# One-hot planes made for half a pair at once, and groups and matrices cut by chunk, in a graph network on one core

## The chip, the cores and the metric
One core of one Trainium2 chip runs the whole kernel. The metric is the device time of one execution in microseconds. A change is judged by the median of several executions of each kernel.

## The reference
A graph of 3125 nodes with 128 features has 103125 edges (src, dst), sorted by dst, each with a weight and six attributes. Four blocks follow each other, each ending in a layer normalisation of x plus the block's output:

```
0: h = x + segsum(x[src], dst);      out = x @ Wres + bres + relu(h @ W1 + b1) @ W2 + b2
1: twice: h + mean over edges of h[src], then two linear maps and a relu
2: four steps: x + 0.1 * tanh(x @ A.T + neighbours(x @ W_phi.T) + self + bias)
   neighbours: sum over edges of dinv[src] * dinv[dst] * edge_weight * h[src]
3: relu(segsum((x @ W + b)[src] + (edge_attr @ We + be), dst))
```

That is eight sums over the edges of the same graph: 1 + 2 + 4 + 1.

## The kernel before
The kernel turns the edges into two dense 3125 x 3125 matrices once: counts (fp16) and weights (float32), with the self loops taken in. Each of the eight sums is then a dense product on TensorE. The nodes are laid out as node = 25 p + k, with p one of 125 partitions and k one of NC = 25 chunks. A chunk of destinations is 125 columns of a matrix; a source chunk k is 125 rows.

**Build.** A pair is two destination chunks (PAIRS = 13, the last one half empty). For a pair every one of 125 destinations t has up to 64 slots of edges for each of its two chunks, on 128 partitions. VectorE makes one-hots in `produce`: `hot_hi`, 128 wide, from the source's partition (L660), `eq`, LO = 26 wide, from its chunk (L658), and eq times the two halves of the weight (L665, two multiplies). All are fp16. This goes in STEPS = 4 steps of 34, 33, 33 and 25 destinations; two buffers alternate, so step u waits (`sums_ok`) until TensorE has used step u - 2. TensorE (`pair`, L1304) multiplies hot_hi by the three narrow planes, four small products for a destination, in UNITS = 15 units of 8 or 9 destinations, and between the units it does the sums of round 0 for the pair before, ten products at a time (`sum_counts`, L1279). ScalarE (`leave`, L962 and L964) copies each unit out of one of three PSUM slots to a staging buffer, counts and weights. There are two staging buffers. SyncE's queue (L391 to L401) waits for the counts of a pair and stores them in `count_mats` (L395), waits for the weights and stores them in `weight_mats` (L398), waits until both have landed and only then hands the buffer back with `stg_free`, for which ScalarE waits at the start of a pair. The pairs are a loop: the first is written out on TensorE, the other twelve are a loop body.

**Rounds.** Round 0 has its sums from the build and goes through product1, product2, normalisation and transposes, group by group. In the seven others TensorE runs `aggregate` for one group of destination chunks after another: GROUPS = 7 groups, six of GRP = 4 chunks (500 columns, one PSUM bank) and one of one chunk. Layers 1 and 3 (rounds 1, 2, 7) read the counts in fp16 (L1183): 25 source chunks, each as a high and a low part, so 50 products a group; ten of them, then product1 of the group before, ten more, product2 of the group before, twenty in a loop whose addresses come from registers, and the last ten. The four rounds of layer 2 (3 to 6) read the weights in float32 (L1193): 25 products, which the trace shows as 50 passes. The matrices come from DRAM through a ring of four slots, two pairs (four chunks) to a load; a weight group is two loads (source chunks 0 to 12 and 12 to 25). SyncE issues load i when item i - 4 is used; the first load of round 7, in a counts slot over two weight slots, waits for one item more (`over_w`). The first group of a round waits for the results of all groups of the round before, piece by piece (`need_parts`). VectorE does `first_sum` and `finish`, ScalarE tanh, square roots and the copies of the transposes.

The code's order is written out by hand; nothing is planned by a scheduler.

Of the kernel before, what the change touches and what calls it, by code (L numbers as in the profile page):

```python
# [31 lines left out]
NODES = 3125  # L32
EDGES = 103125
D = 128
# [19 lines left out]
STEPS = len(STEP_AT) - 1  # L54
SUM_BANK = 7
GRP = 4
GROUPS = -(-NC // GRP)
# [20 lines left out]
def chunks_of(g):  # L78
    return min(GRP, NC - GRP * g)
# [6 lines left out]
def build_program(nc, x, edge_pairs, edge_w, dst_blocks, edge_feats, w, out):  # L86

    ctx = ExitStack()
    with ctx:
# [7 lines left out]
        count_mats = nc.dram_tensor("count_mats", (PAIRS, 128, NC * 2 * NP), F16).ap()  # L97
        weight_mats = nc.dram_tensor("weight_mats", (PAIRS, 128, NC * 2 * NP), F32).ap()
# [95 lines left out]
        stg_c = [at(37500 * i, 128, [NC, 2 * NP], F16) for i in range(2)]  # L194
        stg_w = [at(37500 * i + 12500, 128, [NC, 2 * NP]) for i in range(2)]
# [16 lines left out]
        ring_c = [at(25000 * i, 128, [2, NC, 2 * NP], F16) for i in range(RING)]  # L212
        ring_w = [at(50000 * (i // 2) + (24000 if i % 2 else 0), 128, [2, W_KS[i % 2][1] - W_KS[i % 2][0], 2 * NP])
# [6 lines left out]
        Cn = at(128992, NP, [GROUPS * GRP, D])  # L220
# [129 lines left out]
        def _(sp):  # L350
# [17 lines left out]
            def store_out(g):  # L368
# [3 lines left out]
                sp.dma_start(out.rearrange("(p c) f -> p c f", c=NC)[:, GRP * g:GRP * g + n, :],  # L372
# [14 lines left out]
            def fast_loads():  # L387
# [5 lines left out]
                with sp.Fori(0, PAIRS) as q:  # L393
                    sp.wait_ge(counts_out, UNITS * q + UNITS)
                    sp.dma_start(count_mats[bass.ds(q, 1)].rearrange("a p n -> (a p) n"),  # L395
                                 stg_all[:, bass.ds(q % 2, 1), 0:STG_C // 2].bitcast(F16).rearrange("p a n -> p (a n)")).then_inc(mats_out, 16)
                    sp.wait_ge(weights_out, UNITS * q + UNITS + OUT_PAD)
                    sp.dma_start(weight_mats[bass.ds(q, 1)].rearrange("a p n -> (a p) n"),  # L398
                                 stg_all[:, bass.ds(q % 2, 1), STG_C // 2:].rearrange("p a n -> p (a n)")).then_inc(mats_out, 16)
# [6 lines left out]
                full = NC // GRP  # L406
                sp.dma_start(inv_deg[:, 0:full, 0:GCOL],
                             row[:, 0:full * GCOL].rearrange("o (g n) -> o g n", n=GCOL).to_broadcast([D, full, GCOL])).then_inc(inv_in, 16)
                sp.dma_start(inv_deg[:, full, 0:NODES - full * GCOL],
                             row[:, full * GCOL:].to_broadcast([D, NODES - full * GCOL])).then_inc(inv_in, 16)  # L410
# [93 lines left out]
        def _(dve):  # L504
# [140 lines left out]
            def produce(q, u):  # L645
# [4 lines left out]
                def code(cols, wide):  # L650
                    return cols.rearrange("p q t j -> p (q t) j").unsqueeze(2).to_broadcast([128, n, wide // 2, 2])
# [773 lines left out]
```

## Time and profile before

| | |
|---|---|
| time, median of 3 | 1177.41 us (1174.58 to 1179.05) |
| profiled execution, its time and its span | 1174.85 us, 1173.0 us |
| granted TensorE clock, mean | 0.96 |
| TensorE busy | 1044.1 us (89%) |
| VectorE busy | 543.5 us (46%) |
| ScalarE busy | 274.7 us (23%) |
| moved by DMA | 310.57 MB, 265 GB/s on the mean |
| chain that ended last | TensorE 75%, DMA 12%, VectorE 5% |

Times inside the span are us from its start. The build lies between about 88 and 312, round 0 between 312 and 343; the float32 rounds are from 501 to 1083, the last round ends at 1173. Busy shares are means over these stages, which have different limits. The granted clock is a share of 2.4 GHz.

### The profile page before, as it was taken

Reading aid. Unit: us, or ns where it says so; the run is one execution under the profiler, and the core shown is the slowest. Engines: PE = TensorE matmul, PEld = TensorE weight load, DVE = VectorE, ACT = ScalarE, POOL = GpSimd, SP = SyncE. Lnnn points to the kernel's source line nnn. Section 1 sums busy time; section 2 is a strip of 40 time slices with the busy share of each in tenths; the row PEclk is TensorE's granted clock in tenths of the full one; section 3 lists DMA queues with packets and bytes.
Section 4 is the critical chain, followed back from the end, with each engine's and each line's share of the span. In section 5 each row is a group of like instructions: output and inputs, shape, how many; then the busy total and the mean of one; then the engine's idle time right before and its main releaser. Section 6 shows DMA issues by size and latency. Waiting matters only on the chain.

```text
span 1173.0 us, 25340 instructions
## 1 busy us (share of the span) xinstructions
PE 1044.1 (89%) x10553; PEld 619.7 (53%) x10553; DVE 543.5 (46%) x1061; ACT 274.7 (23%) x558; POOL 67.8 (6%) x69
## 2 busy tenths in 40 slices
PE   0335888888869999999999999999999999999998
PEld 0234677777655555545445554465544645445454
DVE  4398799999473336522312223222322314444333
ACT  0246698888520000000000000000000002112100
POOL 3811000000000000000000000000000000000000
PEclk9865799999999999999999999999999999999999
DMA  6405476767798675777766987669886698753951
GB/s 190 104 12 157 202 299 287 300 287 300 328 367 349 236 303 222 268 304 312 262 254 227 386 354 284 233 247 382 337 305 222 258 385 324 306 203 145 427 193 31
DMA packets 40520, 310.57 MB, mean 265 GB/s; under 512 B 12138, under 2 KB 15069, under 8 KB 18581
## 3 DMA queue, kind: packets, MB, share of 16 engines
q1 hardware_dynamic: 29528, 299.34, 65.0%
q0 software_dynamic: 8416, 9.50, 2.9%
q10 hardware_dynamic: 2522, 0.98, 0.4%
q8 instruction: 38, 0.62, 0.2%
q14 instruction: 16, 0.13, 0.0%
HBM read 244.49 MB, written 65.26 MB: 264 GB/s over the span
## 4 chain that ended last, share of the span: by engine, by line
PE 75%; DMA 12%; DVE 5%; issue 3%; ACT 2%; ACTq 2%; SPq 0%; DVEq 0%
PE ps L1193 45%; PE ps L1183 17%; DMA weight_mats<-arena 11%; PE ps L1142 4%; PE ps L1304 2%; PE ps L1279 2%; PE ps L1097 2%; PE ps L1155 1%; ACTq L908 1%; DMA edge_table<-arena 1%; ACTq L911 1%; DVE arena L665 1%; PE ps L1124 0%; DVE stats L673 0%; ACT arena L930 0%
## 5 line engine op out<-in xcount | busy, mean ns | idle before, releaser
L1193 PE MATMUL ps<-arena 125*128 125x500 f32 (+1 forms) x700 | 268.5, 539 | 0.0
L1193 PE MATMUL ps<-arena,parts_even 125*128 125x500 f32 (+1 forms) x700 | 267.6, 538 | 0.0
L1193 PEld LDWEIGHTS ps<-arena 125*128 125x128 f32 x700 | 123.3, 190 | 127.8 <-issue 127.8
L1193 PEld LDWEIGHTS ps<-arena,parts_even 125*128 125x128 f32 x700 | 122.9, 189 | 127.4 <-issue 127.4
L948 ACT ACTIVATE XT<-ps 128x500 f32<-128x500 f32 (+1 forms) x49 | 26.6, 543 | 517.8 <-PE ps L1155 517.8
L1183 PE MATMUL ps<-arena 125*128 125x500 f16 (+2 forms) x700 | 140.8, 352 | 3.8 <-issue 3.2
L1304 PE MATMUL ps<-arena 64*128 64x52 f16 (+1 forms) x6500 | 106.5, 181 | 36.5 <-DVE arena L665 21.7
L962 ACT ACTIVATE arena<-ps 128x400 f16<-128x400 f32 (+1 forms) x195 | 124.1, 636 | 38.6 <-PE ps L1304 24.0
L1304 PEld LDWEIGHTS ps<-arena 64*128 64x128 f16 x6500 | 96.4, 95 | 54.3 <-ACT arena L964 30.8
L964 ACT ACTIVATE arena<-ps 128x400 f32<-128x400 f32 (+1 forms) x195 | 116.6, 598 | 0.0
L660 DVE TENSOR_TENSOR arena<-arena 128x4224 f16<-128x4224 f16 (+2 forms) x52 | 116.2, 2235 | 0.0
L784 DVE TENSOR_TENSOR arena<-ps,dinv 125x512 f32<-125x512 f32 (+1 forms) x28 | 17.8, 634 | 197.0 <-PE ps L1142 197.0
L742 DVE COPY arena<-ps 128x500 f32<-128x500 f32 (+1 forms) x28 | 17.4, 621 | 186.5 <-PE ps L1193 186.5
L1183 PEld LDWEIGHTS ps<-arena 125*128 125x128 f16 (+1 forms) x700 | 64.6, 96 | 72.0 <-issue 6.7
L1279 PE MATMUL ps<-arena,parts_even 125*128 (+1 forms) x650 | 86.2, 283 | 2.3 <-ACT x_buf L970 1.8
L497 POOL DMA_INDIRECT arena<-in_edge_feats,ptr x25 | 31.1, 1245 | 886.9 <-DVE S L812 860.8
L1183 PE MATMUL ps<-arena,parts_even 125*128 125x500 f16 (+2 forms) x350 | 71.1, 354 | 0.6 <-issue 0.4
L1279 PEld LDWEIGHTS ps<-arena,parts_even 125*128 125x128 f16 x650 | 60.9, 101 | 12.3 <-ACT arena L962 1.9
L665 DVE TENSOR_TENSOR arena<-arena 128x858 f16<-128x858 f16 (+2 forms) x104 | 55.4, 574 | 0.0
L1183 PEld LDWEIGHTS ps<-arena,parts_even 125*128 125x128 f16 (+1 forms) x350 | 32.8, 97 | 34.1 <-issue 1.7
L1020 ACT ACTIVATE arena<-arena 125x512 f32<-125x512 f32 (+1 forms) x28 | 16.3, 584 | 136.6 <-DVE arena L787 136.6
L658 DVE TENSOR_TENSOR arena<-arena 128x858 f16<-128x858 f16 (+2 forms) x52 | 30.2, 580 | 21.4 <-PE ps L1304 20.5
(176 smaller groups left out, 710.6 us busy)
## 6 DMA issues: line engine op xcount, KB each, us to landing
arena<-weight_mats SPq DMA_DIRECT2D x24, 3250.0 KB, 11.4
arena<-weight_mats SPq DMA_DIRECT2D x24, 3000.0 KB, 10.9
arena<-count_mats SPq DMA_DIRECT2D x18, 3125.0 KB, 13.2
weight_mats<-arena SPq DMA_DIRECT2D x13, 3125.0 KB, 14.4
count_mats<-arena SPq DMA_DIRECT2D x13, 1562.5 KB, 6.0
arena<-weight_mats SPq DMA_DIRECT2D x4, 1625.0 KB, 7.2
arena<-weight_mats SPq DMA_DIRECT2D x4, 1500.0 KB, 6.3
arena<-count_mats SPq DMA_DIRECT2D x3, 1562.5 KB, 6.2
```

Source lines behind the costliest of these rows:

```text
L497: nc.gpsimd.indirect_dma_start(attrs[c % 3].rearrange("p s t -> p (s t)"), None, feats_v, bass.IndirectOffsetOnAxis(ptr8[:, c:c + 1], 1)). ...
L658: v.tensor_tensor(eq, numbers(iota_lo, LO), code(lo_c[:, bass.ds(q, 1), t0:t0 + n, :], LO), ALU.is_equal).then_inc(eq_ok, 1)
L660: v.tensor_tensor(hot_hi[b][:, 0:n, :].rearrange("p t (a j) -> p t a j", j=2), numbers(iota_hi, 128), code(hi_c[:, bass.ds(q, 1), t0:t0 + ...
L665: ins = v.tensor_tensor(to, eq, code(w_c[:, bass.ds(q, 1), t0:t0 + n, k, :], LO), ALU.mult)
L948: s.activation(XT[:, GCOL * g:GCOL * g + n], ps[:, 6 + q % 2, 0:n], ACT.Copy).then_inc(xt_ready, 1)
L962: s.activation(stg_c[odd].rearrange("p k (j t) -> p k j t", j=2)[:, :, :, cols], sums_of(u, 0), ACT.Copy).then_inc(counts_out, 1)
L964: s.activation(stg_w[odd].rearrange("p k (j t) -> p k j t", j=2)[:, :, :, cols], sums_of(u, 1), ACT.Copy).then_inc(weights_out, 1)
L1142: ins = t.matmul(o, a, b[:, :], start=(i == 0 and r != 7), stop=(i == len(terms) - 1), skip_group_check=(r == 7))
L1183: ins = t.matmul(o, lhs, rhs, start=(not loop and k == 0 and j == 0), stop=(not loop and k == NC - 1 and j == 1))
L1193: ins = t.matmul(o, xs[:, k, :], rhs, start=(k == 0), stop=(k == NC - 1))
L1279: ins = t.matmul(o, parts_even[:, j, k, :], counts[:, 2 * NP * k:2 * NP * k + 2 * NP], start=(k == 0 and j == 0), stop=(k == NC - 1 and j ...
L1304: ins = t.matmul(ps[:, bank + j, o + (LO if a else 0):o + 2 * LO], hot_hi[b][rows, e, :], hot_lo[b][rows, e, LO * a:LO * z], start=(T == U ...
```

## The change
- `produce` makes the narrow planes for half a pair (67 and 58 destinations) instead of for a step: one comparison, then one multiply that writes both weight planes, reading eq once for each plane. hot_hi is still made by steps. The order on VectorE is now: wait for the buffers of step 2h, eq of half h, hot_hi of step 2h, multiply of half h (step 2h is then ready), wait for the buffer of step 2h + 1, hot_hi of that step.
- `hot_lo` holds three planes [3, destinations, 26], one buffer for each half; TensorE reads the first two as two pieces of 26.
- The matrices in staging and DRAM are by chunk: [2 chunks, 25, 125] for a pair, where they were [25, 250]. The rows of a store are two pieces of half the length; a load takes up to four chunks, each a piece of its own. Products read pieces of 125 columns where they read 250.
- The groups are 4, 4, 4, 4, 4, 3, 2 chunks. 25 chunks are loaded for a round, where it was 13 pairs.

```diff
+HALF_AT = STEP_AT[::2]
-GROUPS = -(-NC // GRP)
+GROUP_AT = (0, 4, 8, 12, 16, 20, 23, NC)
+GROUPS = len(GROUP_AT) - 1
...
-        count_mats = nc.dram_tensor("count_mats", (PAIRS, 128, NC * 2 * NP), F16).ap()
+        count_mats = nc.dram_tensor("count_mats", (PAIRS, 2, 128, NC * NP), F16).ap()
...
-        hot_hi = [at(75000 + 14008 * i, 128, [STEP_MAX, 128], F16) for i in range(2)]
-        hot_lo = [at(83704 + 14008 * i, 128, [STEP_MAX, 3 * LO], F16) for i in range(2)]
+        hot_hi = [at(75000 + 8704 * i, 128, [STEP_MAX, 128], F16) for i in range(2)]
+        HALF_MAX = max(z - a for a, z in zip(HALF_AT, HALF_AT[1:]))
+        hot_lo = [at(92408 + 10452 * i, 128, [3, HALF_MAX, LO], F16) for i in range(2)]
...
-            def produce(q, u):
-
-                t0, n, b = STEP_AT[u], STEP_AT[u + 1] - STEP_AT[u], u % 2
-                eq = hot_lo[b][:, 0:n, 0:LO].rearrange("p t (a j) -> p t a j", j=2)
+            def produce(q, half):
...
-                used = UNITS_TO[u - 2] - (UNITS if u < 2 else 0)
-                dve.wait_ge(sums_ok, UNITS * q + used + SUMS_PAD)
-                v.tensor_tensor(eq, numbers(iota_lo, LO), code(lo_c[:, bass.ds(q, 1), t0:t0 + n, :], LO),
-                                ALU.is_equal).then_inc(eq_ok, 1)
-                v.tensor_tensor(hot_hi[b][:, 0:n, :].rearrange("p t (a j) -> p t a j", j=2), numbers(iota_hi, 128),
-                                code(hi_c[:, bass.ds(q, 1), t0:t0 + n, :], 128), ALU.is_equal)
-                dve.wait_ge(eq_ok, STEPS * q + u + 1)
-                for k in range(2):
-                    to = hot_lo[b][:, 0:n, LO + LO * k:2 * LO + LO * k].rearrange("p t (a j) -> p t a j", j=2)
-                    ins = v.tensor_tensor(to, eq, code(w_c[:, bass.ds(q, 1), t0:t0 + n, k, :], LO), ALU.mult)
-                ins.then_inc(hots_ok, 1)
+                def wait_used(u):
+
+                    used = UNITS_TO[u - 2] - (UNITS if u < 2 else 0)
+                    dve.wait_ge(sums_ok, UNITS * q + used + SUMS_PAD)
+
+                def rows_hot(u):
+                    t0, n = STEP_AT[u], STEP_AT[u + 1] - STEP_AT[u]
+                    return v.tensor_tensor(hot_hi[u % 2][:, 0:n, :].rearrange("p t (a j) -> p t a j", j=2),
+                                           numbers(iota_hi, n, 128), code(hi_c[:, bass.ds(q, 1), t0:t0 + n, :], 128),
+                                           ALU.is_equal)
+
+                t0, n, u = HALF_AT[half], HALF_AT[half + 1] - HALF_AT[half], 2 * half
+                eq = hot_lo[half][:, 0, 0:n, :]
+                wait_used(u)
+                v.tensor_tensor(eq.rearrange("p t (a j) -> p t a j", j=2), numbers(iota_lo, n, LO),
+                                code(lo_c[:, bass.ds(q, 1), t0:t0 + n, :], LO), ALU.is_equal).then_inc(eq_ok, 1)
+                rows_hot(u)
+                dve.wait_ge(eq_ok, 2 * q + half + 1)
+                both = w_c[:, bass.ds(q, 1), t0:t0 + n, :, :].rearrange("p q t k j -> p (q t k) j")
+                v.tensor_tensor(hot_lo[half][:, 1:3, 0:n, :].rearrange("p k t m -> p t k m"),
+                                eq.unsqueeze(2).to_broadcast([128, n, 2, LO]),
+                                both.unsqueeze(2).to_broadcast([128, 2 * n, LO // 2, 2]), ALU.mult).then_inc(hots_ok, 1)
+                wait_used(u + 1)
+                rows_hot(u + 1).then_inc(hots_ok, 1)
...
-                            if n == GCOL:
-                                rhs = slot[:, :, ks, :].rearrange("p q a n -> p q (a n)")
-                            else:
-                                rhs = slot[:, 0:1, ks, 0:NP].rearrange("p q a n -> p (q a n)")
+                            rhs = slot[:, 0:chunks_of(g), ks, :].rearrange("p c a n -> p c (a n)")
...
-                                                   hot_lo[b][rows, e, LO * a:LO * z],
+                                                   hot_lo[half][rows, a:z, e_lo, :],
```

## Rows read from the trace of the kernel before
**Rows 1.** The page, part 4: share of the chain by line.
```profile
PE ps L1193 45%; PE ps L1183 17%; DMA weight_mats<-arena 11%; PE ps L1142 4%; PE ps L1304 2%; PE ps L1279 2%; PE ps L1097 2%; PE ps L1155 1%; ACTq L908 1%; DMA edge_table<-arena 1%; ACTq L911 1%; DVE arena L665 1%; PE ps L1124 0%; DVE stats L673 0%; ACT arena L930 0%
```
**Rows 2.** Timeline of SyncE's queue: start, duration, what (idle before, releaser).
```profile
133.73 0.35 SPq L395 DMA_DIRECT2D count_mats<-arena  x1
...
292.92 0.34 SPq L395 DMA_DIRECT2D count_mats<-arena  x1
```
**Rows 3.** The chain in order of time, one pair: start, duration, what.
```profile
214.65 14.42 DMA weight_mats<-arena
```
**Rows 4.** Timeline of the build, VectorE, TensorE and ScalarE around 211 us.
```profile
210.31 1.14 DVE L665 TENSOR_TENSOR arena<-arena 128x884 f16<-128x884 f16 x2
...
211.59 0.63 PE L1304 MATMUL ps<-arena 64*128 64x52 f16 x36 [1.34 <-DVE arena L665]
...
212.26 1.24 PE L1279 MATMUL ps<-arena,parts_even 125*128 x10
...
213.45 0.62 ACT L962 ACTIVATE arena<-ps 128x450 f16<-128x450 f32 x1 [1.51 <-SPq L401]
...
214.57 0.62 PE L1304 MATMUL ps<-arena 64*128 64x52 f16 x36 [0.16 <-ACT arena L964]
...
215.35 0.60 DVE L658 TENSOR_TENSOR arena<-arena 128x858 f16<-128x858 f16 x1
...
218.14 1.11 DVE L665 TENSOR_TENSOR arena<-arena 128x858 f16<-128x858 f16 x2
```
**Rows 5.** Groups by form, VectorE's one-hots: busy us, mean ns of one.
```profile
L660 DVE TENSOR_TENSOR arena<-arena 128x4224 f16<-128x4224 f16 x26 | 61.1, 2351 | 0.0
...
L660 DVE TENSOR_TENSOR arena<-arena 128x4352 f16<-128x4352 f16 x13 | 31.5, 2420 | 0.0
...
L660 DVE TENSOR_TENSOR arena<-arena 128x3200 f16<-128x3200 f16 x13 | 23.6, 1818 | 0.0
...
L658 DVE TENSOR_TENSOR arena<-arena 128x884 f16<-128x884 f16 x13 | 8.1, 620 | 2.3 <-PE ps L1304 1.6 <-DVE W_rep L823 0.4
L658 DVE TENSOR_TENSOR arena<-arena 128x650 f16<-128x650 f16 x13 | 6.5, 499 | 10.0 <-PE ps L1304 9.9
```
**Rows 6.** Timeline, TensorE in the second pair and around 195 us.
```profile
123.09 0.35 PE L1304 MATMUL ps<-arena 64*128 64x26 f16 x10 [2.97 <-issue]
...
195.43 0.63 PE L1304 MATMUL ps<-arena 64*128 64x52 f16 x36 [1.56 <-ACT arena L964]
...
195.99 2.27 PE L1279 MATMUL ps<-arena,parts_even 125*128 x10
```
**Rows 7.** Windows: PE, PEld, DVE, ACT, POOL busy; clock, DMA share, GB/s.
```profile
196.00:200.00 4.00, 4.00 (x117) 3.10 (x113) 3.11 (x3) 2.09 (x5) 0.00 (x0) 0.58 0.35 147
...
332.00:336.00 4.00, 2.18 (x16) 1.53 (x15) 3.46 (x16) 1.32 (x3) 0.00 (x0) 1.00 1.02 434
...
502.00:1078.00 576.00, 576.00 (x1854) 298.09 (x1853) 167.01 (x320) 45.01 (x70) 26.68 (x22) 1.00 0.74 284
```
**Rows 8.** Timeline, end of round 6 and start of round 7.
```profile
1075.21 8.86 SPq L422 DMA_DIRECT2D arena<-count_mats  x4
...
1079.19 3.96 PE L1193 MATMUL ps<-arena,parts_even 125*128 125x125 f32 x34
...
1085.69 3.24 PE L1183 MATMUL ps<-arena 125*128 125x500 f16 x10 [2.54 <-issue]
```
**Rows 9.** The page, part 6: KB of one transfer, median us to landing.
```profile
arena<-weight_mats SPq DMA_DIRECT2D x24, 3000.0 KB, 10.9
```
**Rows 10.** The chain in order of time, a float32 group and an fp16 group.
```profile
1014.64 17.61 PE ps L1193 x42
...
1142.19 10.56 PE ps L1183 x50
```
**Rows 11.** Timeline, the looped products of round 1's last group.
```profile
420.56 2.73 PE L1183 MATMUL ps<-arena 125*128 x20 [0.41 <-issue]
```
**Rows 12.** Timeline, the last full group's scaling.
```profile
1166.34 1.11 DVE L682 TENSOR_SCALAR arena<-arena,mv,rstd 125x128 f32<-125x128 f32 x4
```

More of the change, by code:

```diff
@@ L78, in chunks_of, with groups_to @@
 def chunks_of(g):
-    return min(GRP, NC - GRP * g)
+    return GROUP_AT[g + 1] - GROUP_AT[g]
+def groups_to(k):
+    return sum(a < k for a in GROUP_AT[:-1])
 def layer_of(r):
@@ L211, in build_program @@
         RING = 4
-        ring_c = [at(25000 * i, 128, [2, NC, 2 * NP], F16) for i in range(RING)]
-        ring_w = [at(50000 * (i // 2) + (24000 if i % 2 else 0), 128, [2, W_KS[i % 2][1] - W_KS[i % 2][0], 2 * NP])
+        ring_c = [at(25000 * i, 128, [GRP, NC, NP], F16) for i in range(RING)]
+        ring_w = [at(50000 * (i // 2) + (24000 if i % 2 else 0), 128, [GRP, W_KS[i % 2][1] - W_KS[i % 2][0], NP])
                   for i in range(RING)]
@@ L641, in _, with numbers @@
             v.tensor_copy(mode[:, :], ps[0:1, 6, 0:1]).then_inc(mode_ok, 1)
-            def produce(q, u):
-                t0, n, b = STEP_AT[u], STEP_AT[u + 1] - STEP_AT[u], u % 2
-                eq = hot_lo[b][:, 0:n, 0:LO].rearrange("p t (a j) -> p t a j", j=2)
+            def produce(q, half):
                 def code(cols, wide):
+                    n = cols.shape[2]
                     return cols.rearrange("p q t j -> p (q t) j").unsqueeze(2).to_broadcast([128, n, wide // 2, 2])
-                def numbers(row, wide):
+                def numbers(row, n, wide):
@@ L825, in fast @@
                 with dve.Fori(0, PAIRS) as q:
-                    for u in range(STEPS):
-                        produce(q, u)
+                    for half in range(2):
+                        produce(q, half)
                 dve.wait_ge(sq_ok, 1)
@@ L1220, in aggregate @@
                     pe.wait_ge(slot_in[(i + 1) % RING], 16 * ((i + 1) // RING + 1))
-                    for k in range(12, NC, GRP):
-                        need_parts(r, g, min(k + GRP, NC))
-                        ins = weight_steps(slot, 1, range(k, min(k + GRP, NC)))
+                    for a, z in zip(GROUP_AT[3:], GROUP_AT[4:]):
+                        need_parts(r, g, z)
+                        ins = weight_steps(slot, 1, range(a, z))
                     ins.then_inc(item_used, 1)
@@ L1300, in pair @@
                             o, e = 2 * LO * (T - UNIT_AT[u]), T - STEP_AT[step]
+                            half = step // 2
+                            e_lo = T - HALF_AT[half]
                             for a, z in ((0, 2), (2, 3)):
```

100 lines of the change are left out of this document (51 added, 49 removed).

## The prediction, written before the changed kernel had run
> **What bounds the kernel now.** I read the chain of waits first. Nearly half of the span is TensorE in L1193 (the four float32 rounds) and 17% in L1183 (the fp16 rounds); 11% is one transfer, weight_mats<-arena [rows 1]. So there are two stages: the build of the matrices, in 13 passes called pairs, up to about 306 us, and then eight rounds in which TensorE is hardly ever idle. The change touches both.
>
> In the build, SyncE's queue issues the store of a pair's counts every (292.92 - 133.73) / 10 = 15.92 us; the weights' store follows, and the chain waits 14.42 us for it [rows 2, 3]. The rest of the 15.92 is queue work, and ScalarE begins a pair only when the earlier store is in: 1.51 us of idle before the copy at 213.45 [rows 4]. So it is the store that sets the pace.
>
> The timeline of one pair shows what is right behind it: a circle between VectorE and TensorE. VectorE makes the one-hots of a step (33 or 34 of the 125 columns), TensorE multiplies the step's four units and frees the buffer, and VectorE may then make the step after next. With S0 to S3 for the four steps of a pair: S0 is ready at 210.31 + 1.14 = 211.45; TensorE starts 0.14 later and ends unit 3 at 214.57 + 0.62 = 215.19; VectorE begins S2 at 215.35; its last operation ends at 218.14 + 1.11 = 219.25 [rows 4].
>
> **Build, old circle.** Durations are from the rows by form [rows 5]. Between the starts of L658 and L665 lie 218.14 - 215.35 = 2.79 us for operations of 0.60 and 2.35 us, so each next operation starts 0.08 before the recorded end of the last. S2 needs 3.90 us (0.60 + 2.35 + 1.11 - 0.16), S0 needs 0.62 + 2.42 + 1.14 - 0.16 = 4.02. TensorE needs 3.58 us from S0 ready to unit 3 done (3.74 less the 0.16 for ScalarE in the last row), so 3.5 from S2 ready to unit 11 done. With 0.16 from TensorE to VectorE, twice, the circle is 3.58 + 0.16 + 3.90 + 3.52 + 0.16 + 4.02 = 15.3 us. It fits under 15.92 with 0.6 us to spare.
>
> **Build, new circle.** Two halves (67 and 58 columns) replace the four steps for the narrow planes. Removed for a pair: two comparisons of the narrow planes and six of the eight multiplies; the rows_hot operations stay as they are. VectorE's own work falls: eight operations fewer, each with a fixed cost (620 ns for 884 elements, 499 for 650: 0.52 ns an element, so 0.16 fixed, less the overlap of 0.08), 8 x 0.08 = 0.65 us. But the first step of a half now waits for the planes of both steps. At 0.52 ns an element (the wide rows give the same: 2351 - 1818 ns over 1024):
> - comparison of 67 x 26 = 1742 elements: 0.62 + 858 x 0.52 = 1.07 us; of 1508: 0.94;
> - both planes in one multiply, 3484 elements: 1.82 + 284 x 0.52 = 1.97 us; 3016: 1.72.
> So S0 is ready after 1.07 + 2.42 + 1.97 - 0.16 = 5.30 us instead of 4.02, and S2 after 0.94 + 2.35 + 1.72 - 0.16 = 4.85 instead of 3.90. The waits before them are not moved: half 0 still waits for unit 11 of the pair before, half 1 for unit 3. The circle: 3.58 + 0.16 + 4.85 + 3.52 + 0.16 + 5.30 = 17.57 us. S1 and S3 come soon enough (one rows_hot behind S0 and S2), and VectorE is idle in the circle although it has less to do. TensorE waits some 0.7 us before unit 8, and before unit 0 over 2 us (from unit 11 to unit 0 pass 0.16 + 5.30, and units 12 to 14 with their sums fill less than 3 of it). ScalarE (15.92 less its 1.51 of idle, 14.4 us of copies) and the store (15.9) then have slack; that covers also what smaller pieces in the store might cost, up to 1.6 us a pair.
>
> 17.57 - 15.92 = 1.65 us for each of the ten pairs at this pace: 16.5 us. The first two pairs are slower in any case: the clock is at 1.2 GHz and TensorE stands for the code of its loop, as at 123.09 with 2.97 us [rows 6]. There the later first S0 costs 1.3 and the two longer half-productions a part of 2 x (1.28 + 0.95): between 1.3 and 5.8, I take 2.9, because part hides behind the code stalls. Build: +19.4.
>
> **The granted clock.** After a gap of 1.34 us it held in the pair above; after one of 1.56 us TensorE fell to 1.2 GHz (0.58 granted on the mean from 196 to 200), and the ten sums took 2.27 us instead of 1.24 [rows 4, 6, 7]. Today the slack of the pair hides that. In the new circle it would not: about +1.4 us each time (1.0 for the sums, the rest in the units), and the gap before unit 0 is longer. In round 0, where TensorE works 2.18 of 4 us, the full 2.4 GHz held [rows 7], so the bounds are 0 and 12 x 1.4 = 17 us; I take 2, one or two falls.
>
> **Rounds.** Groups of 4,4,4,4,4,3,2 chunks replace six of 4 and one of 1.
> - *End of round 6.* The first matrix of round 7 lies over both weight slots and is loaded only when group 5 is done: issued at 1075.21; TensorE then has the one-chunk group, ends at 1079.19 + 3.96 = 1083.15, and stands 2.54 us until 1085.69; the trace calls it issue, but 1085.69 is 10.5 us behind the load's issue, and loads of about that size land after 10.9 us on the median. The first ten are then slow, 3.24 us where 2.11 is normal (50 take 10.56) [rows 8 to 10]. A last group of two chunks gives 50 x 0.21 = 10.5 us and products: the load is hidden. -2.5 and -1.1 = -3.6.
> - *Float32 passes.* 500 columns take 17.61 / 42 = 0.419 us (34 of the 42 are of this group), 125 columns (3.96 - 0.16) / 34 = 0.112, 0.16 of it the end of the last [rows 8, 10]; a pass over all columns but 2000 costs 0.531 now and 0.524 as 375 + 250 in proportion. 0.007 x 50 x 4 rounds = -1.4.
> - *fp16 passes.* 20 narrow ones in the register-addressed loop take 2.73 us [rows 11], 0.14 to 0.2 each where 0.053 is their share of 0.211. That floor hits now two groups: 375 columns want 0.158 (a loss of up to 0.04 x 20), 250 want 0.106 (0.09 x 20), against 0.14 x 20 before: -0.2 to +1 a round; I take +0.9, three rounds: +2.7. The sources are now pieces of 125 with odd fp16 offsets; no row has that, so nothing to +10 us, I take nothing, as in the nearest row, where 500 columns in two pieces of 250 take 0.211 [rows 10].
> - *Loads* have the same bytes in pieces half as long. The transfer engines are 74% busy in the float32 rounds [rows 7] and each load has four slots' time: hidden until they take a third longer.
> - *Round 0* ends with shorter VectorE work for group 5: -0.8. *Tail:* one chunk more in the last normalisation, 0.28 for the scaling (1.11 for four) [rows 12] and as much again for each other operation: +1.
> Rounds: -3.6 - 1.4 + 2.7 - 0.8 + 1.0 = -2.1.
>
> Sum: 19.4 + 2 - 2.1 = +19.3. The profiled execution took 1174.85 us (span 1173.0); the median of three is 1177.41, 2.6 above it. I forecast 1174.85 + 19.3, and half of the 2.6, as 1195.
>
> The Trainium skill ("VectorE: DVE Perf Modes", the section on the TRN2 errata) says that each VectorE instruction on SBUF pays a fixed latency and advises larger tiles to pay it less often. The rows agree on the fixed part (0.16 us a record) [rows 5]. By that rule the change should speed the build; it is rival A, and the circle is why I don't follow it.
>
> **Rivals.**
> A. *VectorE's total is the bound, or the store stays it.* If waits between the two engines overlap more than I read, the pair stays at 15.92 and only the rounds count: 1177.4 - 2 to - 5, so 1174; if VectorE's saving of 0.65 us a pair also went through, 8 us more, 1166. For it: from 210.31 to 219.25 VectorE has no idle time. Against it: ScalarE's 1.51 us behind the store, which no VectorE saving removes [rows 4]. It decides if S0 to S0 stays under 15.92. Chance 0.15.
> B. *The clock falls in nearly every pair.* 17 us instead of 2: 1210. For it: the gap of over 2 us; against it: round 0. Chance 0.2.
> C. *The combined multiply is not at two elements a cycle.* Its source repeats a row for both planes, which no row shows. At twice the time an element (1.04 ns) the two cost 3.4 us a pair more, 12 pairs: 1236. Chance 0.05.
>
> The Trainium skill ("Vector Engine (DVE) Microarchitecture Reference", section 5.1) lists what lets a two-source operation take pairs: 2-byte types and an innermost step of 1; a row read again is allowed. By that C should not happen; no run here shows it yet.
>
> **How the numbers follow.** Forecast 0.6, A 0.15, B 0.2, C 0.05. The forecast's own range is 1186 to 1204 (start of the build 1.3 to 5.8, fp16 passes, circle 16.9 to 17.9). Leaving out C, the end of B and the better part of A: 1176 to 1213. A change within 0.5% (6 us) can't be told from none: A counts half as same and half as faster: slower 0.84, same 0.08, faster 0.08.
>
> **What would show it.** Stores of the counts 17 to 18 us apart; SyncE no longer the one that ScalarE waits for; TensorE waiting over 2 us for the combined multiply before unit 0; the multiply at 1.97 us; no stall at the start of round 7. Wrong if the stores still come every 16 us, if VectorE has no idle time in the build, or if the multiply takes over 3 us.

## The result and the profile after

| | before | after |
|---|---|---|
| median | 1176.89 us (4 runs, 1174.58 to 1179.05) | 1200.6 us |
| ratio | | 1.0193, 95% interval 1.0164 to 1.0223 |
| profiled execution, time and span | 1174.85, 1173.0 us | 1202.75, 1200.9 us |
| last count store of the build issued | 308.46 | 337.82 |
| end of the build (last sums of round 0) | 311.83 | 345.51 |
| start of the first fp16 group of round 1 | 343.36 | 379.62 |
| granted clock, mean | 0.96 | 0.945 |

Slower by 1.9%; 1.0193 of 1176.9 is 1199.6. (A fourth execution of after, of 1321.96 us at a clock of 0.84, is outside the ratio; with it the median of four reads 1200.6.)

The chain by line, to be held against [rows 1]. The transfer weight_mats<-arena, 11% there, is gone from it. VectorE's multiply has grown from 1% (L665) to 4% (L683), TensorE's units from 2% (L1304) to 6% (L1321), the sums of round 0 from 2% (L1279) to 5% (L1294).

```profile
PE ps L1208 44%; PE ps L1201 17%; PE ps L1321 6%; PE ps L1294 5%; PE ps L1163 5%; DVE arena L683 4%; PE ps L1118 2%; PE ps L1176 1%; ACTq L929 1%; DMA edge_table<-arena 1%; ACTq L932 1%; PE ps L1145 0%; DVE stats L694 0%; ACT arena L985 0%; DMA arena<-in_edge_w 0%
```

SyncE's queue of after, the stores of the counts; it answers to [rows 2], where they came every 15.9 us. From 136.51 to 337.82 they come every 201.31 / 11 = 18.30 us, and one interval, 154.71 to 171.70, is 16.99.

```profile
136.51 0.39 SPq L402 DMA_DIRECT2D count_mats<-arena  x1
154.71 0.38 SPq L402 DMA_DIRECT2D count_mats<-arena  x1
171.70 0.38 SPq L402 DMA_DIRECT2D count_mats<-arena  x1
190.41 0.38 SPq L402 DMA_DIRECT2D count_mats<-arena  x1
...
337.82 0.38 SPq L402 DMA_DIRECT2D count_mats<-arena  x1
```

VectorE of after in that pair [rows 4, 5]: start, duration, what, in brackets the idle time before it and what ended it. VectorE stands twice a pair, each time for TensorE, with four operations in each half where it had eight.

```profile
150.88 1.07 DVE L678 TENSOR_TENSOR arena<-arena 128x1742 f16<-128x1742 f16 x1 [1.67 <-PE ps L1321]
151.86 2.42 DVE L671 TENSOR_TENSOR arena<-arena 128x4352 f16<-128x4352 f16 x1
154.20 1.96 DVE L683 TENSOR_TENSOR arena<-arena 128x3484 f16<-128x3484 f16 x1
...
159.61 0.95 DVE L678 TENSOR_TENSOR arena<-arena 128x1508 f16<-128x1508 f16 x1 [1.18 <-PE ps L1321]
...
162.74 1.72 DVE L683 TENSOR_TENSOR arena<-arena 128x3016 f16<-128x3016 f16 x1
...
167.87 1.07 DVE L678 TENSOR_TENSOR arena<-arena 128x1742 f16<-128x1742 f16 x1 [1.67 <-PE ps L1321]
```

TensorE of after, start of three pairs. Before unit 0 it stands 3.05 us for L683, each time; at 156.30 the clock holds (ten sums in 1.25 us), in the next two pairs it doesn't (2.26 us).

```profile
156.30 0.62 PE L1321 MATMUL ps<-arena 64*128 64x52 f16 x36 [3.05 <-DVE arena L683]
156.85 1.25 PE L1294 MATMUL ps<-arena,parts_even 125*128 x10
158.03 1.43 PE L1321 MATMUL ps<-arena 64*128 64x52 f16 x100
...
164.59 1.02 PE L1321 MATMUL ps<-arena 64*128 64x52 f16 x68 [0.85 <-DVE arena L683]
...
173.29 0.81 PE L1321 MATMUL ps<-arena 64*128 64x52 f16 x36 [3.05 <-DVE arena L683]
174.03 2.26 PE L1294 MATMUL ps<-arena,parts_even 125*128 x10
...
191.99 0.68 PE L1321 MATMUL ps<-arena 64*128 64x52 f16 x36 [3.05 <-DVE arena L683]
192.59 2.26 PE L1294 MATMUL ps<-arena,parts_even 125*128 x10
```

Two windows of after, columns as in [rows 7]: the build has a mean clock of 0.88, and the stretch around that gap 0.50.

```profile
155.00:300.00 145.00, 115.70 (x4400) 96.38 (x4400) 111.94 (x64) 110.48 (x247) 0.00 (x0) 0.88 0.64 265
...
172.00:176.00 4.00, 2.71 (x46) 2.02 (x46) 3.42 (x2) 1.09 (x3) 0.00 (x0) 0.50 0.86 350
```

End of round 6 in after: the stall of [rows 8] is gone, and the first ten products of round 7 take 2.29 us, not 3.24. But inside the first group of round 7 there is a new wait of 1.29 us, for VectorE's results of the last group, which now has two chunks.

```profile
1106.05 7.34 PE L1208 MATMUL ps<-arena,parts_even 125*128 125x250 f32 x34
1113.23 2.29 PE L1201 MATMUL ps<-arena 125*128 125x500 f16 x10
...
1124.41 4.43 PE L1201 MATMUL ps<-arena 125*128 125x500 f16 x20 [1.29 <-DVE arena L718]
```

**Where the 27.9 us between the two profiled spans are.** From the tables of both traces:

| stretch | us |
|---|---|
| before the first of the stores that count (133.73, 136.51) | +2.8 |
| eleven pairs at 16.99 instead of (308.46 - 133.73) / 11 = 15.88 | +12.2 |
| the same pairs beyond 16.99 (lower clock) | +14.4 |
| last pair: in before its counts were ready some 2.2 us before SyncE, waiting for the earlier store, issued theirs; in after there is no such slack | +2.6 |
| last fifty sums (7.21 instead of 5.54, lower clock) | +1.7 |
| round 0, from its first product (33.6 instead of 31.0) | +2.6 |
| rounds 1 and 2 (154.3 instead of 158.15) | -3.9 |
| rounds 3 to 6 | -2.3 |
| stall at the start of round 7 | -2.5 |
| round 7 | +0.3 |

The profiled execution of after, 1202.75 us, is the slowest of the three in the ratio (the others took 1196.62 and 1198.45), so these 27.9 us are more than the 22.7 of the ratio. Two of the rows are falls of the clock that come and go from one profile to the next: in the kernel with one more operation beside the circle (below), whose build is otherwise the same, the last fifty sums take 5.54 us and round 0 takes 31.3.

### The profile page after: what moved, and what is told of

It is laid out like the page before. It is cut to its first block, busy times and chain, and to the rows that moved or that the text cites. A ratio compares the mean times of both kernels' runs of the same rounds, so it can differ in the third digit from the quotient of the medians.

```text
span 1200.9 us, 25107 instructions
## 1 busy us (share of the span) xinstructions
PE 1053.9 (88%) x10553; PEld 645.3 (54%) x10553; DVE 536.1 (45%) x957; ACT 276.6 (23%) x558; POOL 68.5 (6%) x69
## 4 chain that ended last, share of the span: by engine, by line
PE 81%; DVE 8%; issue 5%; ACT 2%; ACTq 2%; DMA 1%; DVEq 0%; SPq 0%
PE ps L1208 44%; PE ps L1201 17%; PE ps L1321 6%; PE ps L1294 5%; PE ps L1163 5%; DVE arena L683 4%; PE ps L1118 2%; PE ps L1176 1%; ACTq L929 1%; DMA edge_table<-arena 1%; ACTq L932 1%; PE ps L1145 0%; DVE stats L694 0%; ACT arena L985 0%; DMA arena<-in_edge_w 0%
## 5 line engine op out<-in xcount | busy, mean ns | idle before, releaser
L1208 PE MATMUL ps<-arena,parts_even 125*128 125x500 f32 (+2 forms) x700 | 267.5, 537 | 0.0
L1208 PE MATMUL ps<-arena 125*128 125x500 f32 (+2 forms) x700 | 267.5, 537 | 0.0
L1321 PE MATMUL ps<-arena 64*128 64x52 f16 (+1 forms) x6500 | 106.8, 183 | 59.0 <-DVE arena L683 52.8
L969 ACT ACTIVATE XT<-ps 128x500 f32<-128x500 f32 (+2 forms) x49 | 26.6, 542 | 511.3 <-PE ps L1176 511.3
L1201 PE MATMUL ps<-arena 125*128 125x500 f16 (+3 forms) x700 | 139.6, 352 | 1.7 <-DVE arena L718 1.3
L1321 PEld LDWEIGHTS ps<-arena 64*128 64x128 f16 x6500 | 97.1, 97 | 77.6 <-issue 52.4
L805 DVE TENSOR_TENSOR arena<-ps,dinv 125x512 f32<-125x512 f32 (+2 forms) x28 | 17.8, 634 | 202.5 <-PE ps L1163 202.5
L1294 PE MATMUL ps<-arena,parts_even 125*128 (+1 forms) x650 | 96.9, 305 | 1.9 <-ACT x_buf L991 1.9
L763 DVE COPY arena<-ps 128x500 f32<-128x500 f32 (+2 forms) x28 | 17.4, 623 | 175.6 <-PE ps L1208 175.6
L1294 PEld LDWEIGHTS ps<-arena,parts_even 125*128 125x128 f16 x650 | 65.2, 108 | 16.6 <-ACT arena L983 2.0
L1201 PE MATMUL ps<-arena,parts_even 125*128 125x500 f16 (+3 forms) x350 | 70.6, 352 | 0.3 <-issue 0.3
L678 DVE TENSOR_TENSOR arena<-arena 128x1742 f16<-128x1742 f16 (+1 forms) x26 | 26.2, 1007 | 54.6 <-PE ps L1321 54.1
L683 DVE TENSOR_TENSOR arena<-arena 128x3484 f16<-128x3484 f16 (+1 forms) x26 | 47.9, 1843 | 0.0
L1041 ACT ACTIVATE arena<-arena 125x512 f32<-125x512 f32 (+2 forms) x28 | 16.4, 584 | 136.4 <-DVE arena L808 136.4
```

What stands on the lines that cost most here:

```text
L678: v.tensor_tensor(eq.rearrange("p t (a j) -> p t a j", j=2), numbers(iota_lo, n, LO), code(lo_c[:, bass.ds(q, 1), t0:t0 + n, :], LO), ALU. ...
L683: v.tensor_tensor(hot_lo[half][:, 1:3, 0:n, :].rearrange("p k t m -> p t k m"), eq.unsqueeze(2).to_broadcast([128, n, 2, LO]), both.unsque ...
L969: s.activation(XT[:, NP * GROUP_AT[g]:NP * GROUP_AT[g] + n], ps[:, 6 + q % 2, 0:n], ACT.Copy).then_inc(xt_ready, 1)
L1201: ins = t.matmul(o, lhs, rhs, start=(not loop and k == 0 and j == 0), stop=(not loop and k == NC - 1 and j == 1))
L1208: ins = t.matmul(o, xs[:, k, :], rhs, start=(k == 0), stop=(k == NC - 1))
L1294: ins = t.matmul(o, parts_even[:, j, k, :], counts[:, :, k, :], start=(k == 0 and j == 0), stop=(k == NC - 1 and j == 1), skip_group_check ...
```

## The experiments

Two theories were on the table. *Circle*: VectorE and TensorE wait for each other, and every microsecond between a freed buffer and the next S0 or S2 lengthens the pair; the clock falls in the gap this opens on TensorE. *Total*: the combined operations themselves, VectorE's sum of work or the new layout cost the time. The measured ratios are to the kernel before, run on the same chip in the same job.

| kernel | median us | ratio, 95% interval |
|---|---|---|
| half-pair planes alone | 1204.77 | 1.0247 (1.0221 to 1.0274) |
| changed kernel | 1200.6 | 1.0193 (1.0164 to 1.0223) |
| changed, one more operation beside the circle | 1199.42 | 1.0203 (1.0178 to 1.0228) |
| changed, the same operation on the circle | 1225.93 | 1.0432 (1.0405 to 1.0459) |
| changed, gap filled | 1183.52 | 1.0067 (1.0048 to 1.0087) |
| layout by chunk alone | 1180.68 | 1.0036 (1.0021 to 1.0052) |
| layout and groups, four old steps | 1172.22 | 0.9970 (0.9958 to 0.9982) |
| changed, narrow planes early | 1169.13 | 0.9941 (0.9920 to 0.9962) |
| before, two stores in flight | 1172.98 | 0.9971 (0.9956 to 0.9986) |
| early planes, two stores | 1168.66 | 0.9932 (0.9909 to 0.9955) |
| early planes, two stores, gap filled | 1161.82 | 0.9882 (0.9863 to 0.9900) |

### The change taken apart

**The one-hots back to four steps.** `produce` and the buffers are those of before, all else is the changed kernel:

```diff
-                    for half in range(2):
-                        produce(q, half)
+                    for u in range(STEPS):
+                        produce(q, u)
```

> The changed kernel with its one-hots made by four steps a pair again, as before; the groups of 4,4,4,4,4,3,2 chunks and the matrices by chunk stay. Theory (the circle between VectorE and TensorE, lengthened by the half-pair planes, is what costs in the build): the counts' stores come 15.9 us apart again (18.3 in the changed kernel), the build ends at 312, and the rounds keep what they gained (some 5.8 us between the end of the build and the last instruction): 1176.9 - 5.8 = 1171 us, 0.995 of before. Rival (the pieces of half the length in the stores, or the counts read back as two pieces with odd offsets in the sums, slow the build): the stores stay 17 us or more apart and the time is 1190 or more.

Measured: 1172.22 us, 0.997. The counts' stores are (312.58 - 135.77) / 11 = 16.07 us apart. So the build's loss is the half-pair production's, and the rest of the change is a small gain. The stores are still 0.2 us a pair further apart than in before, which is the layout's doing (next run).

**The groups back too.**

```diff
-GROUP_AT = (0, 4, 8, 12, 16, 20, 23, NC)
+GROUP_AT = (0, 4, 8, 12, 16, 20, 24, NC)
```

> The same with the groups of before too (six of 4 chunks and one of 1), so that of the change only the matrices' layout by chunk is left. If the rounds' gain is the groups' alone: the stall of 2.54 us at the start of round 7 is back, rounds 1 and 2 take 158.2 us instead of 154.3, and the time is that of before, 1176 to 1178, ratio 0.999 to 1.001. If the layout brings part of it (the gain in rounds 1 and 2): 1172 to 1174, ratio 0.997.

Measured: 1180.68 us, 1.0036: neither case. The layout by itself is no gain but costs 0.0036 x 1175.5 = 4.2 us, and the groups are then worth (1.0036 - 0.9970) x 1175.5 = 7.8 us by the ratios (8.5 by the medians), not 5.8. The pieces do cost: the stores are (311.12 - 134.27) / 11 = 16.08 us apart (15.88 in before), fifty fp16 products of 500 columns in four pieces of 125 take 10.66 us (10.56 in two of 250 [rows 10]), 42 float32 passes 17.64 (17.61). A fifty in the chain of this kernel:

```profile
1122.39 10.66 PE ps L1189 x50
```

**The half-pair planes alone.** The kernel before with the new `produce` and its buffers, layout and groups as they were.

```diff
-                    for u in range(STEPS):
-                        produce(q, u)
+                    for half in range(2):
+                        produce(q, half)
...
-                                                   hot_lo[b][rows, e, LO * a:LO * z],
+                                                   hot_lo[half][rows, a:z, e_lo, :],
```

> The kernel before with the half-pair planes and combined multiplies alone; layout and groups of before. Circle theory: stores 18.3 us apart, TensorE waits 3 us for the combined multiply before unit 0 and its clock falls in nearly every pair; the build ends at 345 and the rounds gain nothing: 1200.6 + 5.8 = 1206 us, 1.025 of before. Rival (the loss needs the new layout): below 1190 us.

Measured: 1204.77 us, 1.0247, stores (335.53 - 134.26) / 11 = 18.30 us apart. 2.5% of loss by this part, less the 0.3% that the others bring, is 2.2%; the whole change measured 1.9%, with overlapping intervals. The theory that the loss needs the layout is out.

### Circle or total

**One operation more, beside the circle.** `spare` is a cell that nothing reads.

```diff
                 rows_hot(u + 1).then_inc(hots_ok, 1)
+                v.tensor_reduce(spare, hi_c[:, 0:3, :, :].rearrange("p q t j -> p (q t j)"), AX, ALU.max)
```

> The changed kernel with one more VectorE operation (a reduction that nothing reads, an estimated 0.86 us) behind the last operation of each half, where VectorE then waits for TensorE: two a pair, some 1.7 us of VectorE work. Circle theory: it lies in VectorE's idle time (1.2 and 1.7 us) and moves nothing, 1200 us, 1.020 of before, at most 3 us more. Rival (VectorE's total is the bound in the build): 1.7 us for each of twelve pairs, 1220, 1.038.

Measured: 1199.42 us, 1.0203 (changed kernel 1.0193). VectorE works 1.86 us more in each pair (0.93 an operation) and nothing gets longer. Its timeline shows where they went: 0.82 us of idle time are left of 1.67.

```profile
182.78 0.93 DVE L689 TENSOR_REDUCE arena<-arena 128x1 f16<-128x750 f16 x1
184.53 1.07 DVE L679 TENSOR_TENSOR arena<-arena 128x1742 f16<-128x1742 f16 x1 [0.82 <-PE ps L1323]
```

**The same operation on the circle.**

```diff
+                v.tensor_reduce(spare, hi_c[:, 0:3, :, :].rearrange("p q t j -> p (q t j)"), AX, ALU.max)
                 dve.wait_ge(eq_ok, 2 * q + half + 1)
```

> The same operation put in front of the combined multiply instead, inside the circle, two a pair. Circle theory: each pair is longer by the whole of both, 1.7 us (pairs 17.0 to 18.3 become 18.7 to 20.0): 12 x 1.7 = 20 us more than the changed kernel, 1220 us, 1.037 of before. Rival (VectorE's total): as with the operation behind the half, whatever that gives.

Measured: 1225.93 us, 1.0432, so 0.0229 x 1176.8 = 27 us more than beside the circle, where 20 were expected. The same work costs nothing or 27 us by its place alone. The stores come (361.55 - 137.68) / 11 = 20.35 us apart, beside the circle (336.25 - 136.21) / 11 = 18.19. Of these 2.16 us a pair 1.7 are the operations' own; the other 0.5, some 5 us in eleven pairs, go with the clock: the gap before unit 0 is now 3.05 + 0.84 = 3.89 us, the clock falls behind it in all eleven pairs (in nine of eleven beside the circle), and in this one the second ten sums are slow as well.

```profile
180.83 0.81 PE L1323 MATMUL ps<-arena 64*128 64x52 f16 x36 [3.89 <-DVE arena L685]
181.57 2.26 PE L1296 MATMUL ps<-arena,parts_even 125*128 x10
...
185.63 1.90 PE L1296 MATMUL ps<-arena,parts_even 125*128 x10
```

**The circle cut.** The narrow planes are made ahead of the wait for hot_hi's buffer; for their own buffer they wait (`wait_lo`) for the unit of the pair before that read it last, 7 or 14.

```diff
-                wait_used(u)
+                wait_lo()
...
-                rows_hot(u)
                 dve.wait_ge(eq_ok, 2 * q + half + 1)
...
-                                both.unsqueeze(2).to_broadcast([128, 2 * n, LO // 2, 2]), ALU.mult).then_inc(hots_ok, 1)
+                                both.unsqueeze(2).to_broadcast([128, 2 * n, LO // 2, 2]), ALU.mult)
+                wait_used(u)
+                rows_hot(u).then_inc(hots_ok, 1)
```

> The changed kernel, but the narrow planes of a half are made before the wait for the buffer of the wide one-hots: they wait only for the units that read the half's own planes in the pair before (unit 7 for half 0, unit 14 for half 1), and only the 2.42 or 2.35 us of the wide one-hots are left between TensorE and S0 or S2. Circle theory: the circle falls from 17.0 to some 12 us (3.58 + 0.16 + 2.35 + 3.52 + 0.16 + 2.42), and the store is the bound again: counts' stores 16.0 us apart, the clock at 1.00, 1170 to 1172 us, 0.996 of before, as with the four old steps. VectorE's total (14.15 us busy a pair) stays below the store's 16.0, so its 0.65 us a pair less is worth nothing. Rival (it is the combined operations themselves, or VectorE's total, that cost): stores 17 us or more apart, 1185 or more.

Measured: 1169.13 us, 0.9941; stores (308.82 - 131.77) / 11 = 16.10 us apart. The same combined operations, in another order, cost nothing: it is not what they take, it is where they stand. The circle is not as short as expected, though. From a timeline of the kernel with two stores (below): unit 7 frees hot_hi's second buffer, VectorE then has the last step's rows, both planes of the next pair and its first rows to do, 222.32 to 229.5, and only then can unit 0 start; TensorE needs the other 7.5 us to its next unit 7. That circle is 15 us (the 12 us expected had looked at hot_hi's first buffer alone).

### What the clock costs

**The gap filled.** Ten products that nothing reads, in the 3.05 us in which TensorE stands.

```diff
                         if UNIT_AT[u] == STEP_AT[step]:
+                            if u == 0 and counts is not None:
+                                for _ in range(10):
+                                    t.matmul(ps[:, 6, 0:500], parts_even[:, 0, 0, :],
+                                             parts_even[:, 1, 0:4, 0:125], start=True, stop=True)
```

> The changed kernel plus ten fp16 products of 500 columns (0.21 us each, 2.1 us in all) into a free bank of PSUM before unit 0 of pairs 1 to 12, in the 3 us in which TensorE stands there. They are work beside the reference's. If the clock's fall is a cost of its own on top of the circle: granted 1.00 throughout, the ten sums at 1.25 us instead of 2.20, a pair at 17.0 us instead of 18.3, 13 to 16 us less than the changed kernel: 1185 to 1188, 1.008 of before. If the fall costs nothing beside the circle (VectorE would be waited for all the same), or if it comes from something else than the gap: 1200, as the changed kernel, or a few us more.

Measured: 1183.52 us, 1.0067, so (1.0193 - 1.0067) x 1176.9 = 14.8 us less than the changed kernel. Stores (322.91 - 136.09) / 11 = 16.98 us apart, every one; sums at 1.25 us; granted clock 1.00 where it was 0.88. TensorE does 2.1 us more a pair and the pair is 1.3 us shorter. A timeline of this kernel:

```profile
202.62 2.29 PE L1313 MATMUL ps<-parts_even 125*128 125x500 f16 x10
205.60 0.62 PE L1325 MATMUL ps<-arena 64*128 64x52 f16 x36 [0.70 <-DVE arena L683]
206.16 1.25 PE L1294 MATMUL ps<-arena,parts_even 125*128 x10
```

And a window of it, as the first of after above, with the clock at 1.00:

```profile
155.00:300.00 145.00, 131.36 (x4834) 104.36 (x4827) 121.05 (x69) 119.23 (x266) 0.00 (x0) 1.00 0.71 292
```

### What lies behind the store

**Two stores in flight, in the kernel before.** SyncE hands a staging buffer back when the store of the pair before has landed, not its own; one semaphore for each buffer, and the 13 passes written out.

```diff
-                    sp.wait_ge(mats_out, 32 * q + 32)
-                    sp.sem_inc(stg_free, 1)
+                    if q:
+                        sp.wait_ge(landed[(q - 1) % 2], 32 * ((q + 1) // 2))
+                        sp.sem_inc(stg_free, 1)
```

> The kernel before with the stores of two pairs in flight and nothing else: the old circle by itself. The prediction gave it as 15.3 us a pair right behind the store's 15.92. If so: stores of the counts 15.3 us apart, a gain of 0.6 for each of ten pairs, 1171 us, 0.995 of before. If the circle was read too short (16 or more): no gain, 1177. If it was read too long (waits between the engines overlap more): the pair falls to ScalarE's 14.5, 1163, 0.988.

Measured: 1172.98 us, 0.9971; stores (304.25 - 133.76) / 11 = 15.50 us apart, of two kinds: 15.0 (seven) and 16.3 to 16.4 (four). SyncE is gone from ScalarE's waits, so the store did set the pace; what lies right behind it is 15.0, not the 15.3 of the prediction. In three of the seven pairs of 15.0 us TensorE stands before unit 0 for VectorE (1.30 to 1.35 us), in the other four for ScalarE's copy L968 (1.44 to 1.53). So the old circle between VectorE and TensorE is no longer than 15.0 us, but this run doesn't show that it alone sets them.

```profile
211.37 0.32 SPq L397 DMA_DIRECT2D count_mats<-arena  x1
226.44 0.32 SPq L397 DMA_DIRECT2D count_mats<-arena  x1
242.82 0.32 SPq L397 DMA_DIRECT2D count_mats<-arena  x1
```

The longer kind is again the clock's: behind a gap of 1.55 us the ten sums take 2.27.

```profile
226.91 0.63 PE L1308 MATMUL ps<-arena 64*128 64x52 f16 x36 [1.55 <-ACT arena L968]
227.47 2.27 PE L1283 MATMUL ps<-arena,parts_even 125*128 x10
```

**Early planes and two stores.** The same edit on top of the early planes:

```diff
+                wait_lo()
...
+                        sp.wait_ge(landed[(q - 1) % 2], 32 * ((q + 1) // 2))
```

> The same with the stores of two pairs in flight: SyncE lets ScalarE have a staging buffer when the store of the pair before is in, not its own pair's, with a semaphore for each of the two buffers; its 13 passes are written out. If what makes the pair 16.0 us is that the store must land before the next is issued: ScalarE's copies (13.9 us busy a pair, 14.4 with their waits) or VectorE's 14.15 are the next bound, 14.5 us a pair, ten pairs give 15 us: 1156, 0.983 of before. Rival (the transfer itself is the bound, 4.69 MB a pair at the 300 GB/s of today): stores still 15.3 us or more apart, 1165 to 1172.

Measured: 1168.66 us, 0.9932, no better than early planes alone (the intervals overlap almost wholly). Neither case: the transfer is not the bound, since four stores come 15.05 us apart, but the other seven come 15.8 to 16.3 apart, and the mean is (307.61 - 134.62) / 11 = 15.73. TensorE stands 1.90 us before unit 0, for the rows that now close the circle. Timeline of that kernel:

```profile
222.32 1.83 DVE L680 TENSOR_TENSOR arena<-arena 128x3200 f16<-128x3200 f16 x1 [1.61 <-PE ps L1331]
...
227.17 4.69 DVE L680 TENSOR_TENSOR arena<-arena 128x4352 f16<-128x4352 f16 x2
...
229.73 0.62 PE L1331 MATMUL ps<-arena 64*128 64x52 f16 x36 [1.90 <-DVE arena L680]
```

**The same with the gap filled,** by seven products instead of ten.

```diff
+                                for _ in range(7):
```

> Early planes and two stores in flight, plus seven fp16 products of 500 columns (1.5 us, beside the reference's work) in the 1.9 us in which TensorE stands before unit 0. In that kernel without them the counts' stores came 15.05 us apart where the clock held and 16.1 where it fell behind this gap, seven of eleven. If the fall is the whole difference: all pairs at 15.05, 7 x 1.05 = 7 us less, 1161 us, 0.987 of before. If the long pairs have another cause (the transfer): 1168, as without.

Measured: 1161.82 us, 0.9882: the fastest kernel here, faster than the one before and the changed one. All stores are (298.91 - 133.71) / 11 = 15.02 us apart and the clock holds at 1.00. The seven products compute nothing that is used; the gain is 1.2% against before and 3.0% against the changed kernel.

```profile
133.71 0.36 SPq L404 DMA_DIRECT2D count_mats<-arena  x1
...
298.91 0.36 SPq L404 DMA_DIRECT2D count_mats<-arena  x1
```

## Why the prediction was right, and where it was wrong

The sign, the mechanism in the build (the circle comes out from behind the store) and the time (1195 against 1199.6 by the ratio) were right. That the time came so close is in part luck. The sum hides four errors of size: the circle was put 5.8 us too long over its ten pairs and the groups' gain 5.7 us too small, the clock 12.8 us and the layout 4.2 us too cheap.

- **Store as the bound, circle behind it: right.** SyncE was what ScalarE waited for, and no longer is; VectorE waits for TensorE and TensorE for L683. The pair of experiments with one operation in two places shows the circle directly.
- **The operations' durations: right.** The multiply takes 1965 and 1722 ns where 1.97 and 1.72 us were worked out, the comparisons 1067 and 946 (1.07, 0.94). S0 is ready after 154.20 + 1.96 - 150.88 = 5.28 us (5.30), S2 after 162.74 + 1.72 - 159.61 = 4.85 (4.85). Rival C is out, and the rule of the page "Vector Engine (DVE) Microarchitecture Reference" of the Trainium skill, section 5.1, that a row read again does not slow a two-source operation, is borne out by those 1965 ns.
- **TensorE's part of the circle: 0.28 us too long, twice.** From S0 ready to VectorE's next start are 159.61 - 156.16 = 3.45 us (3.74 in the prediction), from S2 ready 167.87 - 164.46 = 3.41 (3.68). The figure was read from a pair of before in which TensorE stood for ScalarE in front of unit 3, and only the 0.16 us that the row names were taken off [rows 4]. But records back to back overlap by some 0.06 us and more; the 64 and 36 products with that wait between them took 215.19 - 213.43 = 1.76 us, the 100 without it 1.43. And from the start of unit 0 to the ten sums passed 212.26 - 211.59 = 0.67 us there, 156.85 - 156.30 = 0.55 here. So the circle is 16.99, not 17.57, and the old one by the same count 3.45 + 3.90 + 3.41 + 4.02 = 14.8, not 15.3; the kernel before with two stores, at 15.0, allows that and rules 15.3 out. Ten pairs: +10.7 by the prediction's count (16.99 - 15.92), not +16.5.
- **The first pairs: right.** +2.9 predicted, the store at 133.73 is at 136.51.
- **The clock: the step that failed.** "I take 2, one or two falls" of a range of 0 to 17. Of the eleven pairs from 138 to 321 us ten have their first sums at 1.97 to 2.26 us, one at 1.25; the filled gap puts the price of the falls at 14.8 us. Rival B was the truth about this term, and it had been given 0.2. The reason against it was round 0, where TensorE stands often at the full 2.4 GHz; but at its end, in the kernel before, is a row that the prediction did not read: behind a gap of 2.66 us the products take 0.63 us instead of 0.38.

```profile
339.57 0.76 PE L1142 MATMUL ps<-sb_L_W,arena 128*125 128x128 f32 x2 [2.66 <-ACT arena L941]
340.12 0.64 PE L1142 MATMUL ps<-sb_L_Wres,XT 128*125 128x128 f32 x2
```

  Nor is a gap under 1.4 us safe, as the pair of [rows 4] with its 1.34 suggests. Two pairs on in the same trace the clock falls behind 1.31 us (granted 0.72 on the mean from 242 to 246), and behind other gaps of 1.31 us, at 258.77 and 274.26, it holds.

```profile
242.65 0.63 PE L1304 MATMUL ps<-arena 64*128 64x52 f16 x36 [1.31 <-DVE arena L665]
243.34 1.92 PE L1279 MATMUL ps<-arena,parts_even 125*128 x10
```

  The nearest rows, that one and the fall behind 1.56 us [rows 6], spoke for B. B's 1210 came out too high only because the circle was shorter and the rounds gained more.
- **Groups: in part right at the end of round 6, wrong in the fp16 passes.** The stall of 2.54 us and the slow ten products went, as forecast. But the new wait of 1.29 us for the two-chunk group's results takes some of it back: from the end of round 6 to the second ten products of round 7's second group pass 1129.11 - (1106.05 + 7.34) = 15.7 us instead of 1101.31 - 1083.15 = 18.2, so -2.4, not -3.6. Float32 rounds are 144.95 us instead of 145.40 in the same layout (-0.45 each, -0.35 forecast). But fp16 rounds are not 0.9 slower; rounds 1 and 2 take 506.17 - 347.43 = 158.74 us with the old groups and 502.40 - 347.73 = 154.67 with the new, 2.0 us less for each. TensorE's timeline at the end of round 1, with the layout by chunk and six groups of 4 and one of 1:

```profile
420.88 0.72 PE L1189 MATMUL ps<-arena 125*128 125x125 f16 x10
422.33 1.11 PE L1151 MATMUL ps<-L_W,arena 128*125 128x128 f32 x8 [0.73 <-DVE arena L746]
423.27 1.47 PE L1189 MATMUL ps<-arena 125*128 x10
425.22 2.71 PE L1189 MATMUL ps<-arena 125*128 x20 [0.48 <-issue]
427.77 2.29 PE L1189 MATMUL ps<-arena,parts_even 125*128 125x500 f16 x10
```

  The same place with 4, 4, 4, 4, 4, 3, 2:

```profile
419.13 1.24 PE L1189 MATMUL ps<-arena 125*128 125x250 f16 x10
420.21 0.82 PE L1151 MATMUL ps<-L_W,arena 128*125 128x128 f32 x6
420.86 1.28 PE L1189 MATMUL ps<-arena 125*128 x10
422.54 3.21 PE L1189 MATMUL ps<-arena 125*128 x20 [0.41 <-issue]
425.59 2.29 PE L1189 MATMUL ps<-arena,parts_even 125*128 125x500 f16 x10
```

  The last forty products of the one-chunk group took 427.77 - 420.88 = 6.89 us, those of the two-chunk group 425.59 - 419.13 = 6.46, with twice the columns: at 125 columns a product is not paid by the column, and there was a wait of 0.73 us for VectorE that 250 columns cover. The prediction took its floor (0.14 us and more in the loop) to hit the 375-column group as well; it does not, and 250 columns take 0.153 there (3.05 / 20), 0.05 above their share of 0.107. The sum also took the new groups at one floor and the old group at another: with 0.14 for all, 0.034 x 20 is lost where 0.087 x 20 was (-1.1 a round), with 0.2 for all 0.042 x 20 and 0.094 x 20 where 0.147 x 20 was (-0.2). Either way it is a gain, and +0.9 could not have come out. ("All columns but 2000" in the float32 passes should read 2500; the figures there are for the 625 that are left and are right.) The groups are worth 7.8 us of gain in all, where 2.1 stood in the sum for all the rounds.
- **The layout: not nothing.** +4.2 us (1.0036) in place of 0, inside the 0 to 10 that were kept open: 0.2 us a pair in the store and 2 ns a product.
- **Round 0 and the last pair: left out or wrong.** Round 0 was put at -0.8 and is 2.6 us longer between the two profiles. Its clock falls behind gaps of 2.16 and 2.03 us and holds behind two of 1.82 (in before it falls once, behind the 2.66); in the half-pair kernel, where it falls nowhere in round 0, the round takes 29.4 us. So the stretch at 2.4 GHz on which the case against B rested does not stand for the whole round. The last pair's 2.6 us, slack that was there only while the store set the pace, stood nowhere in the sum.

```profile
352.91 0.79 PE L1163 MATMUL ps<-sb_L_W,arena 128*125 128x128 f32 x2 [2.16 <-ACT arena L962]
```

- **Rival A is out.** VectorE's smaller total did come (0.65 us a pair forecast; 14.15 us busy a pair in the kernel with the filled gap, 14.78 with four old steps), but the build is longer. The Trainium skill's advice ("VectorE: DVE Perf Modes", the TRN2 errata) of fewer, larger instructions is borne out as to VectorE's own time only: in the order that keeps the planes off the circle the same operations give 0.9941 where the four old steps give 0.9970, with intervals that touch; in the changed kernel's order they cost 2%.

By parts: circle +10.7, first pairs +2.8, clock +14.8, groups -7.8, layout +4.2 give +24.7; measured +22.7, interval 19.3 to 26.2. (The layout's 0.2 us a pair were measured where the store sets the pace. In the changed kernel it doesn't, which would take some 2 us off; that was not measured.)

What stays open: why the clock holds behind some gaps of 3.05 us and falls behind others of the same length with the same work ahead of it. And what sets the 15.02 us of the fastest kernel: the circle through hot_hi's second buffer closes there (TensorE waits 0.16 us for the rows, VectorE 0.47 for unit 7), but the kernel before with two stores comes to the same 15.0 us with the old order, and there TensorE waits for ScalarE's copies before unit 0 in four of the seven pairs (1.44 to 1.53 us) and ScalarE for TensorE (up to 0.63 us), so a circle of these two through the PSUM slots may lie there too. It was not taken apart.

## What to carry to other kernels

Merging small operations saves the engine that runs them, but it moves work ahead of the first result. Before merging, draw the circle of waits (buffer free, produce, consume, buffer free) and ask which of the merged pieces could be made before the wait; here that order alone was worth 2.5%. Where a gap on TensorE opens on a path that sets the pace, count the clock's fall as the likely case and not as an accident. A last group so narrow that its products are no longer paid by the column is worth splitting more evenly.

## What the runs showed of the hardware that was not expected

- The clock fell behind gaps of 1.31 and 1.55 us as well as 3.05, and held behind others of 1.31, 1.53 and 3.05. A fall costs 1.2 to 1.7 us of the pair: ten sums at 2.26 instead of 1.25 us, and part of the units.
- Products that nothing reads were cheaper than idle time: 2.1 us of them a pair shortened the pair from 18.3 to 16.98 us.
- A VectorE reduction of 750 elements took 929 ns (0.86 was the estimate), against 1965 ns for a two-source multiply of 3484.
- An fp16 product of 500 columns whose moving operand is four pieces of 125 instead of two of 250 takes 10.66 / 50 = 0.2132 us instead of 0.2112.
